# Adding up the top-2 experts on GpSimd, and another order of work in the expert stage and the fp4 stage

## What is computed

```python
def _L1_ffn_ref(tokens, gate_w, expert_w, expert_b, combine_w):
    logits = jnp.einsum('bsh,eh->bse', tokens, gate_w)
    probs = jax.nn.softmax(logits, axis=-1)
    top2_w, top2_idx = jax.lax.top_k(probs, 2)
    ...
    expert_out = jax.nn.silu(jnp.einsum('nh,edh->ned', flat, expert_w) + expert_b[None, :, :])
    gathered = jnp.take_along_axis(expert_out, flat_idx[:, :, None], axis=1)
    mixed = jnp.sum(gathered * flat_w[:, :, None], axis=1)
    out = jnp.einsum('bsh,dh->bsd', mixed.reshape(B, S, H), combine_w)

def fp4_quant_dequant(x):          # blocks of 16 along the last dim
    scale = jnp.max(jnp.abs(xb), axis=-1, keepdims=True) / 6.0
    scale = jnp.maximum(scale, jnp.float32(1e-12))
    xn = xb / scale
    idx = jnp.searchsorted(_MID, jnp.abs(xn))
    q = _GRID[idx] * jnp.sign(xn) * scale

# fp4_linear(x, w) = x quantized times w quantized; the stage is
# w_down of silu(w_gate x) * (w_up x), with 352 hidden units
```

## Time and profile before

| | |
|---|---|
| median of 3 runs | 6254.8 us (6252.84 to 6261.8) |
| the profiled execution | 6261.56 us, of it 6259.8 us span |
| expert stage (from its first mixed product to its last residual add) | 4755 to 5038 us of the span |
| fp4 stage (from the first hidden block scaled to the last) | 5651 to 5934 us of the span |

### The profile page before, as it was taken

One profiled execution on the slowest core, in us unless ns is written; L12 is line 12 of the kernel. 1 busy time (PEld: TensorE's weight loads), 2 busy tenths in 40 slices (PEclk: granted clock), 3 DMA queues, 4 the chain that ended last, 5 costly groups with the idle time before them and its releaser, 6 DMA issues. The chain is left out here.

```text
span 6259.8 us, 121332 instructions
## 1 busy us (share of the span) xinstructions
PE 5663.6 (90%) x38029; PEld 3508.3 (56%) x38029; DVE 4182.8 (67%) x9572; ACT 2815.0 (45%) x4608; POOL 2135.9 (34%) x3000
## 2 busy tenths in 40 slices
PE   7997999999997899879997999889988989886677
PEld 5664444444443677457754776467754556634464
DVE  6875666666665788358854886378835656578764
ACT  4553222222222455535553555445554645533344
POOL 5661000000000666146632665166610012253312
PEclk9998999999998999989998999999998999987799
DMA  4332222222223656046622564066600000000002
GB/s 133 103 106 98 97 96 98 95 96 98 99 94 89 165 155 160 9 121 158 157 63 68 155 160 116 7 165 157 157 13 5 0 7 0 1 4 0 0 2 62
DMA packets 526329, 527.02 MB, mean 84 GB/s; under 512 B 55699, under 2 KB 436706, under 8 KB 503781
## 3 DMA queue, kind: packets, MB, share of 16 engines
q1 hardware_dynamic: 517684, 517.90, 29.7%
q10 hardware_dynamic: 8320, 5.25, 0.4%
HBM read 337.88 MB, written 185.07 MB: 84 GB/s over the span
## 5 line engine op out<-in xcount | busy, mean ns | idle before, releaser
L362 DVE TENSOR_REDUCE a_mx<-a_unit 128x2 f32<-128x512 f32 (+1 forms) x1920 | 1288.2, 686 | 411.8 <-PE a_unit L564 405.5
L468 ACT ACTIVATE a_prob<-a_slot 128x1536 f32<-128x1536 f32 x640 | 928.5, 1451 | 643.3 <-PE a_slot L587 503.4
L562 PE MATMUL a_unit<-a_sk,a_sq 96*128 96x256 bf16 (+3 forms) x5120 | 746.0, 250 | 75.8 <-DMA a_sk<-a_kscratch 41.2
L1177 ACT ACTIVATE f_silu<-f_pG 128x512 f32<-128x512 f32 x528 | 314.8, 598 | 935.0 <-PE f_pG L1252 921.0
L564 PE MATMUL a_unit<-a_maskq,identb 128*128 128x256 bf16 (+1 forms) x1920 | 602.1, 314 | 0.0
L1119 DVE TENSOR_TENSOR f_gated<-f_spread,f_silu 128x512 f32<-128x512 f32 x512 | 354.5, 692 | 351.1 <-ACT f_silu L1177 307.0
L1229 PE MATMUL f_pO<-f_hidden,f_wd 128*128 128x512 f32 x1056 | 545.7, 598 | 13.8 <-DVE f_hidden L1121 13.3
L1252 PE MATMUL f_pG<-f_xnT,f_wg 128*128 128x512 f32 x1056 | 541.1, 594 | 0.0
L1256 PE MATMUL f_pU<-f_xnT,f_wu 128*128 128x512 f32 x1056 | 540.2, 593 | 0.0
L562 PEld LDWEIGHTS a_unit<-a_sk,a_sq 96*128 96x128 bf16 (+1 forms) x5120 | 384.2, 99 | 277.2 <-DVE a_mx L362 154.2
L306 POOL TENSOR_SCALAR_AFFINE_SELECT a_prob<-a_prob 128x512 f32<-128x512 f32 x480 | 309.5, 645 | 578.0 <-ACT a_prob L468 561.4
(11 more groups left out here) (409 smaller groups left out, 11173.0 us busy)
## 6 DMA issues: line engine op xcount, KB each, us to landing
f_spread<-f_scratch SPq DMA_DIRECT2D x1024, 128.0 KB, 2.9
a_sq<-a_qscratch SPq DMA_DIRECT2D x128, 768.0 KB, 5.8
a_sk<-a_kscratch SPq DMA_DIRECT2D x160, 384.0 KB, 6.6
a_qscratch<-a_parts SPq DMA_DIRECT2D x288, 192.0 KB, 2.3
a_qscratch<-a_parts SPq DMA_DIRECT2D x288, 128.0 KB, 2.2
a_kscratch<-a_parts SPq DMA_DIRECT2D x160, 192.0 KB, 2.4
a_kscratch<-a_parts SPq DMA_DIRECT2D x160, 128.0 KB, 2.2
a_qscratch<-a_parts SPq DMA_DIRECT2D x288, 64.0 KB, 1.8
```

The source lines that it names most:

```text
L362: v.tensor_reduce(dst, src, op=ALU.max, axis=AX.X, negate=True).then_inc(red_done, 1)
L468: act.activation(prob[gr % 2][:, :], slot[:, :], ACT.Exp, scale=SCALE).then_inc(exp_done, 1)
L562: pe.matmul(bank[:, at * wide:(at + 1) * wide], q, sk[b][0:KM, gr * GH + h, 0:wide], start=(at == 0), stop=False)
L1177: act.activation(silu[c % 2][:, :], pG[c % 2][:, :], ACT.Silu).then_inc(silu_done, 1)
```

## The change

In the expert stage:
- The five slices are added on GpSimd (`add_parts`): two slices to two (128x256), then one to one, then the fifth, into `whole[t]`. TensorE turns `whole[t]` with one transpose in place of five products. Whoever reuses `part[t]` waits for `whole_done` in place of the turn.
- `b3` and `ones3` have 128 rows, of which 125 rows of `b3` are zero, so the bias product is a 128-row one.
- On TensorE, for each t: experts, then combine the tile turned one t earlier, then turn. The transposes of block n+2 move from t = 2 to t = 3.
- On VectorE statistics come first in a step, ahead of mix 0, and the residual add comes last, behind mix 3.
- `piped` unrolls five steps at the front instead of three.

In the fp4 stage:
- The product `xq` moves from GpSimd to VectorE, right behind `rounded(yx)`, and both stand ahead of `rounded(yh)`.
- GpSimd does, in a step, `hq` of n-1, `yx` of n+2, then 1/sqrt of n+3.
- On TensorE all four turns of block n-1 and their down products are laid between the gate and up products of m, and the transposes of `xq` (now of n+2) end the step. ScalarE follows: silu 3 stands ahead of the norm, and the copy `xqT` ends the step.

```diff
@@ top2_experts, gpsimd
+                def add_parts(n, t):
+                    q = n * BT + t
+                    g.wait_ge(part_done, q + 1)
+                    g.wait_ge(mixed_done, q + 1)
+                    if later(n, 1):
+                        g.wait_ge(m_pe, q + 1 - DEEP)
+                    chain.link(g.tensor_tensor(quarter[:, :, :], part[t][:, 0:2, :], part[t][:, 2:4, :], op=ALU.add))
+                    chain.link(g.tensor_tensor(third[:, :], quarter[:, 0, :], quarter[:, 1, :], op=ALU.add))
+                    g.tensor_tensor(whole[t][:, :], third[:, :], part[t][:, 4, :], op=ALU.add).then_inc(whole_done, 1)
@@ vector, step
+                    if within(n + 2):
+                        statistics(n + 2)
                     if within(n):
                         mix(n, b, 0)
-                    if within(n + 2):
-                        statistics(n + 2)
...
@@ tensor
                 def turn_mixed(q, t):
-                    pe.wait_ge(mixed_done, q + 1)
-                    pe.wait_ge(part_done, q + 1)
+                    pe.wait_ge(whole_done, q + 1)
...
-                    for e in range(parts):
-                        ins = pe.matmul(pM, part[t % DEEP][:, e, :], ident, start=(e == 0), stop=(e == parts - 1))
-                    ins.then_inc(m_pe, 1)
+                    pe.transpose(pM, whole[t % DEEP][:, :], ident).then_inc(m_pe, 1)
@@ fp4_feed_forward, vector, step
                     product(0)
                     product(1)
+                    if is_block(n + 2):
+                        v.wait_ge(ax_done, n + 3)
+                        rounded(yx[:, :], absx[:, :])
+                        if is_block(n + 1):
+                            v.wait_ge(t_pe, n + 2)
+                        unscaled(flat(xq), yx[:, :], nscx[:, :], BLK).then_inc(xq_done, 1)
                     if is_block(n):
                         v.wait_ge(ah_done, n + 1)
                         rounded(yh[b][:, :], absh[:, :])
                         v.sem_inc(rh_done, 1)
                     product(2)
-                    if is_block(n + 2):
-                        v.wait_ge(ax_done, n + 3)
-                        rounded(yx[:, :], absx[:, :])
-                        v.sem_inc(rx_done, 1)
                     product(3)
@@ scalar, step
                     gate(0)
+                    gate(1)
                     if is_block(n):
                         act.wait_ge(yh_done, n + 1)
                         act.activation(absh[:, :], yh[b][:, :], ACT.Abs, scale=TWO_BITS).then_inc(ah_done, 1)
-                    gate(1)
+                    if is_block(n - 1):
+                        turned_hidden(n - 1, 0)
...
@@ tensor, step
+                    gate_up(0)
+                    gate_up(1)
                     if is_block(n - 1):
+                        turn_hidden(n - 1, 0)
+                        turn_hidden(n - 1, 1)
+                        down(n - 1, 0)
                         turn_hidden(n - 1, 2)
                         down(n - 1, 1)
+                    gate_up(2)
+                    if is_block(n - 1):
                         turn_hidden(n - 1, 3)
                         down(n - 1, 2)
+                    gate_up(3)
+                    if is_block(n - 1):
+                        down(n - 1, 3)
```

More of the change, by code:

```diff
@@ L1293, in top2_experts @@
         prod = [k.sb(f"prod{b}", [P, EV, D]) for b in range(2)]; mixT = k.sb("mixT", [P, D])
+        quarter = k.sb("quarter", [P, 2, D]); third = k.sb("third", [P, D])
+        whole = [k.sb(f"whole{t}", [P, D]) for t in range(DEEP)]
         pT = k.ps("pT", [P, BLK])
@@ L1320, in step @@
                         ln_rstd(g, chain, moments, veps, mhalf, rstd, 1e-5, rstd_done, apart)
+                    for t in range(BT):
+                        if within(n):
+                            add_parts(n, t)
                 piped(g, step)
@@ L1413, in step @@
                         chosen(n + 1, 1 - b)
+                    if within(n):
+                        mix(n, b, 3)
                     if later(n, 1):
                         add_out(n - 1, 1 - b)
-                    if within(n):
-                        mix(n, b, 3)
                 piped(v, step)
@@ L1460, in _ @@
                 pe.wait_ge(w_in, W_IN)
[L1461 removed]
+                pe.wait_ge(setup, 3)
                 ident = core["ident"]
@@ L1502, in step @@
                             ins.then_inc(logit_pe, 1)
+                        if within(n):
+                            experts(n, b, t)
+                        if later(n, 1):
+                            combine(n - 1, (n - 1) * BT + t, 1 - b, t)
                         if back:
                             turn_mixed(n * BT + t - LAG, t - LAG)
-                        if within(n):
-                            experts(n, b, t)
-                        if back:
-                            combine(n if t >= LAG else n - 1, n * BT + t - LAG, b if t >= LAG else 1 - b, (t - LAG) % BT)
-                        if t == 2 and within(n + 2):
+                        if t == BT - 1 and within(n + 2):
                             pe.wait_ge(xn_done, n + 3)
@@ L2028, in step @@
                         act.activation(absx[:, :], yx[:, :], ACT.Abs, scale=TWO_BITS).then_inc(ax_done, 1)
+                    if is_block(n - 1):
+                        turned_hidden(n - 1, 1)
+                        turned_hidden(n - 1, 2)
                     gate(2)
+                    if is_block(n - 1):
+                        turned_hidden(n - 1, 3)
+                    gate(3)
                     if is_block(n + 3):
@@ L2036, in step @@
                         ins.then_inc(xn_done, 1)
-                    gate(3)
-                    if is_block(n):
-                        turned_hidden(n, 0)
-                        turned_hidden(n, 1)
+                    if is_block(n + 2):
+                        act.wait_ge(t_pe, n + 3)
+                        act.activation(xqT[:, :], pT[:, :], ACT.Copy).then_inc(xqT_done, 1)
                     if isinstance(n, int) and n == -3:
@@ L2100, in step @@
                         ins.then_inc(t_pe, 1)
-                    if is_block(n - 1):
-                        down(n - 1, 3)
-                    if is_block(m):
-                        pe.wait_ge(xqT_done, m + 1)
-                    for t in range(BT):
-                        gate_up(t)
-                    if is_block(n):
-                        turn_hidden(n, 0)
-                        turn_hidden(n, 1)
-                        down(n, 0)
                 blocks_by_two(pe, step)
@@ L2505, in piped @@
 def piped(eng, step):
-    step(-2, 0)
-    step(-1, 1)
-    step(0, 0)
-    with eng.Fori(0, (BLOCKS - 4) // 2) as i:
-        step(i * 2 + 1, 1)
-        step(i * 2 + 2, 0)
+    for n in range(-2, 3):
+        step(n, n % 2)
+    with eng.Fori(0, (BLOCKS - 6) // 2) as i:
+        step(i * 2 + 3, 1)
+        step(i * 2 + 4, 0)
     step(BLOCKS - 3, 1)
```

77 lines of the change are left out of this document (34 added, 43 removed).

## The result

The changed kernel takes 6186.7 us (median of 4 runs, 6178.42 to 6191.51) against 6258.3 us of the kernel before (4 runs, 6252.84 to 6265.35) on the same chip: a ratio of 0.9884, with a 95% interval of 0.9866 to 0.9901. The forecast was 6186.

A forecast was written before the change was run, and what follows sets the result against it. TensorE was taken to bound the expert stage, VectorE the fp4 stage. Savings of 33 and 36 us sum to 69, so 6254.8 us becomes 6186 us (chance 0.55), range 6158 to 6215.

The forecast's parts named there:

- TensorE's chain: Fp4 rival: late hT copies make steps 17.4 us, total 6200 us, chance 0.15; sign: waits ahead of product 3 or residual add.
- This choice moves nothing: Expert stage: TensorE needs 11.5 us a block with the padding's gain or 13.5 without, both under VectorE's 13.9.
- The rate of 0.57 us per us of GpSimd: VectorE's loss while both engines work on SBUF operands: 1.82 us to 3.17 us of GpSimd, read in the fp4 stage.
- the places that I named: Expert stage, VectorE work beside GpSimd's adds: another mix, two ranking operations behind mix 2, residual add and x + h; 1.8 us.
- mixes longer than 0.96 us: Expert stage sign: VectorE's mixes would take longer than 0.96 us where GpSimd works.
- whose loss no row shows: Expert stage: VectorE's norm after mix 1, with one tensor input; its loss beside GpSimd could not be read from the profile.
- the rival without contention: GpSimd's short adds cost VectorE nothing: -51 in the expert stage, -39 in fp4, 6165 us; chance 0.13.
- the one with 3.3 us: Rival of full overlap: GpSimd's adds cost VectorE 3.3 us a block, expert block 17.2 us, total 6207 us; chance 0.10.
- VectorE's terms: Fp4 step: 19.48 us less waits 0.44 and 1.09, contention 1.82 and 0.54, plus 0.75 for xq, giving 16.3.
- The chain through the other engines: Fp4 stage: ScalarE's copies and TensorE's turns compete with VectorE's 16.3 us step, so 16.5 was taken; as rival 17.4, chance 0.15.
- The slower rival: TensorE falls to its low clock in the expert stage, 23 us a block; 6290 us, slower than before; chance 0.03.
- the 0.95: Expert stage: a granted TensorE clock below 0.95 was named as a sign that the prediction is wrong.

The follow-up runs named there:

- e3: Changed kernel with the five products of the turn on TensorE again in place of GpSimd's adds and one transpose; 6181.2 us, 0.9863 of the kernel before.
- e10: Changed kernel with the turn's five products on TensorE and a three-row bias product, leaving only the new order in the expert stage; 6221.8 us, ratio 0.9932.
- e2: Changed kernel with the bias product of three rows again in place of 128; 6201.1 us, 0.9895 of the kernel before.
- e5: Changed kernel with only the first of GpSimd's three adds per tile, TensorE turning and adding three slices; 6172.5 us, 0.9866 of the kernel before.
- e4: Changed kernel with ScalarE's copies of the turned hidden tiles 0 and 1 moved forward in the fp4 stage; 6168.6 us, 0.9849 of the kernel before.
- e6: Changed kernel with the normed block's rounding and xq moved behind product 2 on VectorE in the fp4 stage; 6214.6 us, 0.9928 of the kernel before.
- e12: As e9, but the fp4 stage's product xq is done by GpSimd behind 1/sqrt; 6157.8 us, 0.9835 of the kernel before.
- e9: Changed kernel with one GpSimd add per tile and ScalarE's early copies in the fp4 stage; 6159.2 us, 0.9835 of the kernel before.

## Why the prediction was right

**What bounds.** In the expert stage VectorE took over from TensorE, without waits, as said: a block of 16.0 us against 15.8 forecast. In the fp4 stage the roundings of 0.69 us and the missing waits ahead of products 0 and 1 came as said; the wait ahead of product 3, the sign named for TensorE's chain, came too.

**TensorE in the expert stage.** Forecast 11.5 us a block from a turn of at most 0.15 and a half of 1.12 us. Measured 0.11 and 1.08, and from e3 15.19 - 4 x (1.11 - 0.11) = 11.2 (a turn of five products takes 1.11 us there). The padding was priced at 2.0 us a block, e10 and e3 show 2.37. "This choice moves nothing" holds for the steady block (e2, 16.0 us) and misses the single blocks at the low clock, 7 to 11 us in all. What it hid from me is more: I never summed the change without GpSimd. 17.67 - 2.0 = 15.7 us stood in my own numbers and is less than the 15.8 that I forecast with the sums. The padding alone gives the whole gain of the stage (41 us), the sums alone 24, and both together 35, less than the padding alone (e10, e3, e2).

**GpSimd's adds.** Priced 0.63, 0.41 and 0.41 us; undisturbed they take 0.72, 0.46 and 0.45, and up to 0.96, 0.92 and 0.51 where an instruction of VectorE began first. That makes 7.4 us a block, close to the 7.2 forecast. The one that reads 256 columns was taken too low, without harm, since GpSimd binds nothing.

**Contention.** Forecast 1.8 us a block, measured 1.9 (e3). The total is right, the way to it is not. The rate of 0.57 us per us of GpSimd was wrong as a mechanism: e5 takes over half of the adds away and VectorE keeps 1.2 of its losses. Of the places that I named, the two operations of the ranking behind mix 2 (`r_more` and `r_coef`) lose 0.61 us; the products of the mixes and x + h lose nothing (only the sum `r_part` behind mix 1 does, 0.29), and the sign "mixes longer than 0.96 us" did not come. The norm, "whose loss no row shows", loses most, 0.69 us, and the other 256-wide instruction of the ranking, ahead of mix 2, loses 0.28; I had put nothing down for either. Both the rival without contention and the one with 3.3 us fall.

**fp4 stage.** The sum of VectorE's terms was 16.3 us, the short steps take 16.0; of the 0.9 us more that `hq` beside the reduction might have cost, nothing came (it keeps 1.62 us). The chain through the other engines, which I had at 17.4 in every step as a rival and took as 0.2 us in the forecast, binds at 18.1 in every second one or 17.1 in each. The mean is 16.9, and -31 us for the steps in place of -36. Forecast and rival were both half right; e4 shows that the chain is what lay between, 18 us, where the forecast had 15 x 0.2 = 3. That this miss of 15 us hardly shows is luck: the sum took 16.5, which comes from a middle step of 19.48 us, away from 18.9, the mean of 15 steps with shorter ones at both ends, a base that is 0.58 us a step too low. With the chain out of the way e4 gives 283.6 - 234.4 = 49 us for the steps, where the prediction's 16.3 gave 39. So what VectorE gains was put 10 us too low, and that covered 10 of the 15 us. The contention taken out by the new order was put at 1.82 us a step, and e6 gives back 1.71. The product `xq`, put at 0.75 us a step for VectorE, takes 0.69 in its row, but e12 against e9 shows that with it on GpSimd a step is no shorter, it is 0.2 us longer.

**The sum.** -38 in the expert stage for -33, where blocks of 16.0 us would give less: 15 x 1.7 = 25. The first blocks are shorter than the steady ones (14.6 to 15.5 us) and the last is 12.7, so the ends gave some 13 us and not 5. In the fp4 stage -31 for the steps, and 6 more in the stage's start and tail. These misses of 3 to 8 us have opposite signs. The two stages gave 75 us where 69 were forecast, and the parts ahead of them, which ended 5 us later, took most of that back; and the kernel before came to 6258.3 us with one run more, where the forecast started from 6254.8. The 6186 owes part of its closeness to all of this.

**The slower rival.** TensorE's clock fell to 0.93 on average in the expert stage, below the 0.95 that I had named as a sign of being wrong, and cost nothing in the steady blocks of the changed kernel, where VectorE never waits. e2 shows the mechanism of that rival at work in two blocks. The rule of the Trainium skill (TensorE: Matmul & The Clock Gate, Part 4) was cited for it, that transposes do not count as products do. The falls that I looked at come behind an idle TensorE (1.38 + 0.44 us in e2, 2.78 in the fp4 stage); no run here tells a transpose from a pause. The nearest pair is e5, which turns a tile with three products, and e2, which turns it with a transpose: from 4860 to 4940 us TensorE is busy for 72.02 and 71.62 us and the clock is 1.00 and 0.93, but the longest wait is 1.02 us in e5 and 1.61 in e2, so the pause differs too.

## What to carry to other kernels

When a change removes load in two ways from the engine that binds, sum each way alone down to the next bound: here the cheap one (a bias product of full height) brought the block to 15.2 us by itself, and the dear one (sums on GpSimd) on top of it moved time to the new bottleneck, 16.0 us. Price GpSimd beside VectorE by pairs, not by a rate: which VectorE instruction with two SBUF inputs, or which norm, begins while a GpSimd instruction runs. Where a copy stands between two turns of one PSUM tile, look what the copying engine has queued ahead of it; two copies moved forward on ScalarE gave 18 us. And take a step's saving from the same kind of step: a middle step from a middle step, a mean from a mean.
